# Start of a Mamba mixer and ternary FFN kernel: first x rows as four loads, per-channel constants turned by TensorE, an epsilon added by GpSimd

## What is computed

```
x = x + mixer(hidden=ctx, z=layernorm(x))          # x: (4, 512, 512), ctx: (4, 512, 256), f32
    xc    = depthwise conv, 4 taps, of in_proj_w @ hidden, + conv_b;   u = silu(xc)       (512 channels)
    x_dbl = x_proj_w @ u  ->  dt_lo (16), B (16), C (16)
    delta = softplus(dt_proj_w @ dt_lo + dt_proj_b);   A = -exp(A_log)
    state = state * exp(delta * A) + (delta * u) * B;   y = state . C     (16 states, 512 steps)
    y     = (y + D * u) * silu(z)
x = x + ffn(layernorm(x))                          # activations rounded to 8 bits, weights to -1, 0, 1
    h = silu(x @ gate) * (x @ up);  h = rms_norm(h) * ln_w;  out = h @ down      (512 -> 2048 -> 512)
```

## Time and profile before

| | |
|---|---|
| runs of before | 584.44 us median (584.33 to 585.72, 3 runs) |
| the profiled execution's own time | 582.04 us |
| its span, first to last instruction | 580.1 us |
| busy share of the span | PE 93%, DVE 92%, ACT 88%, POOL 81% |
| transfers over the whole span | 68.64 MB, mean 118 GB/s |

### The profile page before, as it was taken

The page is one execution under the profiler, slowest core; times in us unless marked ns, Lnnn a source line. Parts: engine busy times, 40 slices in busy tenths (PEclk is TensorE's granted clock), DMA queues, the critical chain, the costliest instruction groups (busy, mean ns, idle before and its releaser), DMA issues.

```text
span 580.1 us, 10283 instructions
## 1 busy us (share of the span) xinstructions
PE 539.6 (93%) x3684; PEld 402.7 (69%) x3684; DVE 534.1 (92%) x774; ACT 512.7 (88%) x755; POOL 468.3 (81%) x197
## 2 busy tenths in 40 slices
PE   5898987899999999999999889898989999999996
PEld 2335476899998989989999889886434444444443
DVE  3999989999999999999999999997899989899873
ACT  1899999999999999989999799998877878878784
POOL 4889374999999899999999999994666665765772
PEclk9999999999999999999999899999999999999999
DMA  9992690112113832117331276253453442533521
GB/s 283 407 373 74 217 315 22 55 56 66 63 56 76 180 82 101 55 56 184 109 93 64 61 180 203 66 137 101 73 98 75 89 103 65 108 82 75 117 54 55
DMA packets 62194, 68.64 MB, mean 118 GB/s; under 512 B 41137, under 2 KB 41137, under 8 KB 59969
## 3 DMA queue, kind: packets, MB, share of 16 engines
q1 hardware_dynamic: 59776, 63.59, 36.7%
q0 software_dynamic: 2368, 4.40, 4.6%
HBM read 50.02 MB, written 8.52 MB: 101 GB/s over the span
## 4 chain that ended last, share of the span: by engine, by line
PE 38%; POOL 18%; ACT 17%; DVE 14%; DMA 7%; issue 5%; SPq 0%; DVEq 0%; POOLq 0%
PE ps L1253 16%; POOL arena L471 16%; PE ps L1263 9%; ACT arena L691 8%; ACT arena L616 5%; PE ps L1218 5%; DVE arena L821 5%; DMA arena<-c_rows 4%; PE ps L1202 4%; PE ps L1205 3%; DVE bst_x L853 2%; DMA arena<-x 1%; ACT arena L613 1%; DVE arena L845 1%; DVE wstat L828 1%
## 5 line engine op out<-in xcount | busy, mean ns | idle before, releaser
L471 POOL TENSOR_TENSOR arena<-arena 128x2048 f32<-128x2048 f32 x63 | 286.7, 4609 | 13.3 <-DVE arena L910 9.8
L910 DVE TENSOR_TENSOR_SCAN arena<-arena,ps 128x512 f32<-128x512 f32 x256 | 286.7, 1195 | 1.7 <-DVE var L935 0.5
L691 ACT ACTIVATE arena<-arena,a_neg 128x512 f32<-128x512 f32 x256 | 165.2, 710 | 9.1 <-DVE arena L910 9.0
L1218 PE MATMUL ps<-ident,arena 128*128 128x128 f32 x1024 | 155.3, 275 | 8.2 <-POOL arena L471 5.0
L1218 PEld LDWEIGHTS ps<-ident,arena 128*128 128x128 f32 x1024 | 120.2, 141 | 12.3 <-POOL arena L471 7.7
L1253 PE MATMUL ps<-arena 128*128 128x512 bf16 x512 | 113.5, 379 | 1.4 <-DVE arena L987 0.9
L511 POOL TENSOR_TENSOR arena<-arena 128x1024 f32<-128x1024 f32 x30 | 70.8, 2362 | 49.9 <-DVE arena L987 49.9
L1202 PE MATMUL ps<-arena 128*128 128x128 f32 x768 | 102.4, 276 | 3.0 <-DVE arena L910 2.8
L1205 PE MATMUL ps<-ident,arena 128*128 128x128 f32 x640 | 97.1, 275 | 5.3 <-DVE arena L910 2.9
L616 ACT ACTIVATE arena<-arena,bT 128x512 f32<-128x512 f32 x160 | 102.0, 709 | 0.0
L1202 PEld LDWEIGHTS ps<-arena 128*128 128x128 f32 x768 | 93.3, 192 | 5.0 <-ACT arena L616 1.9
(11 more groups left out here) (118 smaller groups left out, 573.6 us busy)
## 6 DMA issues: line engine op xcount, KB each, us to landing
arena<-w_all SPq DMA_DIRECT2D x16, 1024.0 KB, 9.5
arena<-c_rows SPq DMA_DIRECT2D x64, 256.0 KB, 3.3
arena<-x SPq DMA_DIRECT2D x4, 1024.0 KB, 15.9
w_ternary<-arena SPq DMA_DIRECT2D x8, 512.0 KB, 4.3
arena<-w_ternary SPq DMA_DIRECT2D x8, 512.0 KB, 5.2
arena<-x POOLq DMA_DIRECT2D x4, 1024.0 KB, 10.0
out<-arena SPq DMA_DIRECT2D x16, 256.0 KB, 2.0
arena<-ctx_t SPq DMA_DIRECT2D x4, 512.0 KB, 13.9
```

The costliest lines, as they stand in the source:

```text
L471: nc.gpsimd.tensor_tensor(hs[:, k % RING, :, :], hs[:, k % RING, :, :], c_bc[:, s:s + 1, :].to_broadcast([P, KE, L]), ALU.mult).then_inc(S ...
L691: nc.scalar.activation(dA[:, s, i, :], delta_u[:, b, 0, i, :], ACT.Exp, scale=a_neg[:, i, n:n + 1]).then_inc(S["dA_ready"], 1)
L910: nc.vector.tensor_tensor_scan(out=hs[:, k % RING, i, :], data0=dA[:, k % 2, i, :], data1=ps[:, 4 + i, :], initial=0.0, op0=ALU.mult, op1= ...
L1218: last = mm(ps[:, c, i * P:(i + 1) * P], hs[:, k % RING, i, c * P:(c + 1) * P], ident[:], start=(n == 0 and i == 0), stop=(n == DS - 1), i ...
```

## The change

SP's two loads for `cw` and `cb` go, and x of batch 0 is issued as four transfers of one row tile, each with its own semaphore; DVE's first `x_stats` waits for one row tile at a time. The taps, bias and D are loaded as rows (channel group by channel, long contiguous pieces) by three DMAs that ACT issues, turned by six transposes on PE into PSUM, and copied by DVE into `chan`; `tap_of` picks a column of it. PE runs nine products of ones ahead of its first `conv`, and DVE sets `ones` and `magic` before it zeroes `xp_s` and `dt_s`. The epsilon for the x variance is added by POOL in place of DVE. POOL's small loads move behind `x_power(0)` (xp_t, now one transfer, and dt) and `x_power(2)` (a_log); xp_t lands in `xp_raw`, and POOL copies it into `xp_s`.

```diff
 SP
-            load(cw[:], conv_w.rearrange("(k p) n -> p k n", p=P), "conv_loaded")
-            with nc.allow_non_contiguous_dma("one column for each channel"):
-                load(cb[:], conv_b.rearrange("(k p) -> p k", p=P), "conv_loaded")
-            load_x(0)
+            for k in range(KE):
+                sp.dma_start(x_all[:, k, :], x_v[:, 0, k, :]).then_inc(x0_loaded[k], 16)
 POOL
-            pool.wait_ge(S["started"], 2)
-            load(xp_s[:, :, 0:DR], xp_v[:, :, 0:DR], "proj_loaded")
-            load(xp_s[:, :, B_AT:XD], xp_v[:, :, DR:DR + 2 * DS], "proj_loaded")
...
             def x_power(b):
                 pool.wait_ge(S["x_var"], b + 1)
+                own.done(nc.gpsimd.tensor_scalar(var_x[:, b, :], mv_x[:, b, :, 1], LN_EPS, None, ALU.add))
+                own.wait()
 ...
             x_power(0)
+            load(xp_raw, xp_t.rearrange("(k p) n -> p k n", p=P), "xp_loaded")
+            pool.wait_ge(S["started"], 2)
...
             x_norm(0)
+            pool.wait_ge(S["xp_loaded"], 16)
+            nc.gpsimd.tensor_copy(xp_s[:, :, 0:DR], xp_raw[:, :, 0:DR]).then_inc(S["proj_ready"], 1)
+            nc.gpsimd.tensor_copy(xp_s[:, :, B_AT:XD], xp_raw[:, :, DR:]).then_inc(S["proj_ready"], 1)
             x_power(1)
             x_norm(1)
             x_power(2)
+            load(a_neg[:], a_log.rearrange("(k p) n -> p k n", p=P), "a_loaded")
 ACT
-            act.wait_ge(S["conv_loaded"], 16 * 2)
+            for at, src in ((0, conv_w.rearrange("(k p) n -> k (p n)", p=P)),
+                            (TAPS * P, conv_b.rearrange("(k p) -> k p", p=P)),
+                            ((TAPS + 1) * P, d_skip.rearrange("(k p) -> k p", p=P))):
+                act.dma_start(chan_rows[:, at:at + src.shape[1]], src).then_inc(S["chan_loaded"], 16)
             act.preload_act_table_set("silu_and_others")
+            act.wait_ge(S["chan_ready"], 1)
             last_tap(0, 0)
 DVE
-                nc.vector.tensor_scalar(var_x[:, b, :], mv_x[:, b, :, 1], LN_EPS, None,
-                                        ALU.add).then_inc(S["x_var"], 1)
+                dve.sem_inc(S["x_var"], 1)
 ...
             x_stats(0)
+            dve.wait_ge(S["chan_psum"], 1)
+            nc.vector.tensor_copy(chan[:], ps[:, 7, 0:(TAPS + 2) * KE]).then_inc(S["chan_ready"], 1)
+            dve.wait_ge(S["chan_ready"], 1)
             conv(0, 0)
 PE
+            pe.wait_ge(S["dve_consts"], 1)
+            keep_warm(9)
             pe.wait_ge(S["in_loaded"], 16)
             conv(0, 0)
+            pe.wait_ge(S["consts_set"], 1)
+            pe.wait_ge(S["chan_loaded"], 16 * 3)
+            for i in range(TAPS + 2):
+                rows = chan_rows[:, i:TAPS * P:TAPS] if i < TAPS else chan_rows[:, i * P:(i + 1) * P]
+                last = nc.tensor.transpose(ps[:, 7, i * KE:(i + 1) * KE], rows, ident[0:KE, 0:KE])
+            last.then_inc(S["chan_psum"], 1)
             conv(0, 1)
```

More of the change, by code:

```diff
@@ L141, in mixer_ffn @@
         a_neg = sb("a_neg", [P, KE, DS])
-        cw = sb("cw", [P, KE, TAPS])
-        cb = sb("cb", [P, KE])
-        dsk = sb("dsk", [P, KE])
+        chan_rows = part(160, 3)[0:KE, :]
+        chan = sb("chan", [P, (TAPS + 2) * KE])
         magic, minus_magic = sb("magic", [P, 1]), sb("minus_magic", [P, 1])
@@ L174, in mixer_ffn @@
         wq_dram = nc.dram_tensor("w_ternary", [8, P, INNER], BF16).ap()
[L176 removed]
+        names = """a_loaded proj_loaded proj_ready in_loaded chan_loaded chan_psum chan_ready xp_loaded started consts_set dve_consts
             in_proj_done tap0_done conv_steps u_ready xdbl_psum xdbl_ready
@@ L187, in mixer_ffn @@
         x_loaded = [sem(f"x_loaded{b}") for b in range(NB)]
+        x0_loaded = [sem(f"x0_loaded{k}") for k in range(KE)]
         x1_added = [sem(f"x1_added{b}") for b in range(NB)]
@@ L251, in added, with tap_of @@
             return "p_added", k * 2 + half + 1 - k // DS
+        def tap_of(i, k):
+            return chan[:, i * KE + k:i * KE + k + 1]
         def flat(ap):
@@ L398, in _, with load @@
             own = Steps(pool, S["pool_steps"])
+            def load(dst, src, s):
+                nc.gpsimd.dma_start(dst, src).then_inc(S[s], 16)
             own.done(nc.gpsimd.memset(ident[:], 0.0))
@@ L411, in _ @@
                                     pattern=[[0, 1]], channel_multiplier=1).then_inc(S["consts_set"], 1)
-            def load(dst, src, s):
-                nc.gpsimd.dma_start(dst, src).then_inc(S[s], 16)
-            xp_v = xp_t.rearrange("(k p) n -> p k n", p=P)
-            pool.wait_ge(S["started"], 2)
-            load(xp_s[:, :, 0:DR], xp_v[:, :, 0:DR], "proj_loaded")
-            load(xp_s[:, :, B_AT:XD], xp_v[:, :, DR:DR + 2 * DS], "proj_loaded")
[L420 to L426, removed]
             def x_power(b):
                 pool.wait_ge(S["x_var"], b + 1)
+                own.done(nc.gpsimd.tensor_scalar(var_x[:, b, :], mv_x[:, b, :, 1], LN_EPS, None, ALU.add))
+                own.wait()
                 nc.gpsimd.tensor_tensor(rstd_x[:, b, :], var_x[:, b, :], mhalf[:, 0:KE],
@@ L450, in _ @@
             x_power(0)
+            load(xp_raw, xp_t.rearrange("(k p) n -> p k n", p=P), "xp_loaded")
+            pool.wait_ge(S["started"], 2)
+            for j in range(2):
+                at = j * XD
+                load(dt_s[at:at + DR, j, :], dt_t, "proj_loaded")
+                load(dt_s[at + DR:at + DR + 1, j, :], dt_b.rearrange("(a n) -> a n", a=1), "proj_loaded")
             x_norm(0)
+            pool.wait_ge(S["xp_loaded"], 16)
+            nc.gpsimd.tensor_copy(xp_s[:, :, 0:DR], xp_raw[:, :, 0:DR]).then_inc(S["proj_ready"], 1)
+            nc.gpsimd.tensor_copy(xp_s[:, :, B_AT:XD], xp_raw[:, :, DR:]).then_inc(S["proj_ready"], 1)
             x_power(1)
@@ L457, in _ @@
             x_norm(3)
-            pool.wait_ge(S["consts_loaded"], 16 * 2)
+            pool.wait_ge(S["chan_ready"], 1)
             for k in range(KE):
-                nc.gpsimd.tensor_scalar(skip[:, k, :], ident[:], dsk[:, k:k + 1], None,
+                nc.gpsimd.tensor_scalar(skip[:, k, :], ident[:], tap_of(TAPS + 1, k), None,
                                         ALU.mult).then_inc(S["skip_ready"], 1)
@@ L800, in step @@
                 own.wait()
+            step(nc.vector.memset(ones[:], 1.0))
+            nc.vector.memset(magic[:], MAGIC).then_inc(S["dve_consts"], 1)
             nc.vector.memset(xp_s, 0.0).then_inc(S["started"], 1)
             nc.vector.memset(dt_s, 0.0).then_inc(S["started"], 1)
-            step(nc.vector.memset(ones[:], 1.0))
-            nc.vector.memset(magic[:], MAGIC).then_inc(S["dve_consts"], 1)
             nc.vector.memset(minus_magic[:], -MAGIC).then_inc(S["dve_consts"], 1)
```

19 lines of the change are left out of this document (12 added, 7 removed).

## The result

The changed kernel took 586.12 us in the median of 22 runs (583.33 to 588.26); the kernel before took 583.59 on the same chip (22 runs, 580.51 to 586.70). The ratio is 1.0044, with an interval of 1.003 to 1.0059: slower, by 2.5 us, where I had forecast 1.9 us faster (582.5), and outside my range of 581.8 to 584.8. The profiled execution took 585.70 us.

The account below looks back on a forecast made before the run. The set-up's chain was taken to bound it: x of batch 0, then DVE alone, with PE's slow projection beside it. DVE's gain of 2.0 and ACT's 1.9, the smaller holding, gave 584.44 - 1.9 = 582.5 us, range 581.8 to 584.8.

Parts of the forecast that it names:

- the 9.9 us for the first projection: Set-up, PE: with its clock up when ctx lands, the first projection is ready at 9.9 us instead of 12.39.
- rival 1: Set-up: PE's clock is still low at 6.2 us, DVE's first tap comes at 15.0, total 585.0 us; chance 0.15.
- When x is there: Set-up: x of batch 0 lands at 9.7 us instead of 10.96, DVE's statistics done at 10.8 (10.0 to 11.6).
- rival 2: Set-up transfers: the stream is not faster, the rate dips being start-up and not small pieces; total 583.4 us; chance 0.15.
- When the taps are there: Set-up: after projection, six transposes (0.8 to 1.1 us) and DVE's copy, DVE's first tap starts at 12.1, 1.9 us earlier.
- What the stream gives back: Set-up: x of batch 2 lands 1.2 us earlier (0.9 to 1.7), so the gain stays 1.9 us (1.6 to 2.1).
- The variance: Set-up, DVE: epsilon taken off its chain saves 0.15 us each for batches 1, 2 and 3.
- POOL: Set-up: its 6.3 us of added work costs nothing, covered by the wait before du(0), 8.25 us, shrinking to about 6.

Follow-up runs that it names:

- c1: The kernel before with 24 small products of ones (96 PE instructions) ahead of PE's first projection; ratio 1.0009.
- c3: The changed kernel with 51 small products of ones added, so PE has 256 instructions more than in the kernel before; ratio 1.0005.
- c4: The changed kernel with 14 products of ones ahead in place of nine and 46 small ones behind, 256 PE instructions more than the kernel before; ratio 1.0002.
- b1_pad: The kernel before with DVE's `ones` set first and 12 products of ones ahead of PE's first projection; ratio 1.0049.
- a1_nowarm: The changed kernel without the nine products of ones ahead of the first projection; ratio 1.0047.
- c2_pad128: The kernel before with 24 small products ahead of PE's first projection and 8 ahead of that of batch 2 (128 PE instructions); ratio 1.0014.
- a0_again: The changed kernel once more, unedited; ratio to the kernel before 1.0067.
- a3: The changed kernel with three later groups of six products of ones cut to two each, 48 PE instructions fewer; ratio 1.0015.
- a2: The changed kernel with the three loads of rows issued by SP ahead of x in place of ACT; ratio 1.0075.
- a4: The changed kernel with 14 products ahead in place of nine and seventeen later ones cut, 4 PE instructions more than the kernel before; ratio 1.0022.

## Why the prediction was wrong

**The step that failed.** "From there the scan and the FFN run as they did, so what the set-up gains or loses is carried to the end one for one". It does not hold: of 3.3 us that the span grew, 2.6 arose behind the third mark, and 0.46 in the scan, where POOL got a second wait for `c_rows`, 0.97 us long. The change lengthens PE's program, and the place at which PE's instructions are loaded then lies in other transfers. I had counted instructions by their time only, not by their number; the earlier trace rows gave me a price for the transposes of PE, and the queue q8 stood on the page before with its 30 packets. That a hit lengthens a pair, and that the number of PE's instructions decides on hits, is shown (long pairs, c1, c3). That undoing the shift takes away the loss in the medians is shown for the changed kernel by c3 (1.0005) and c4 (1.0002). That the long pairs are all of it is not: in b1_pad one long pair costs 0.8 of the 2.1 us by which its span grew, the second wait for `c_rows` is 0.6 more, and the rest is open; a1_nowarm has one long pair and 1.0047, c2_pad128 two and 1.0014.

The second step that failed is in the set-up, 1.9 us forecast and none in this profile: the 9.9 us for the first projection, taken up next. The forecast's base was off as well, the other way: 584.44 us from three runs, where the 22 runs of the kernel before have 583.59.

**The clock: rival 1, in part.** I took 9.9 us for the first projection and kept 12.4. The profile has 12.15 (6.78 + 5.37), a0_again 10.36 and c3_after256 10.28. My reason against, "the gap is 1 us behind 4 us of work", was wrong by size: PE could start on ctx at 6.78 us, 0.6 later than before, the nine products ended at 4.83 and not at 5.3, and the gap was 1.94. With nine products the projection was fast behind gaps of 1.30, 1.75 and 1.83 us (a0, a3, c3) and slow behind 1.94 (after) and 1.02 (a2). So the gap alone does not decide: after 1.94 the clock had been up and fell, in a2 it had not risen yet. The Trainium skill, "TensorE: Matmul & The Clock Gate", section "What you observe", gives some 500 ns from run to run for the point of the rise. Here the same nine products begin at 1.17 us each time, and the traces' clock records begin the higher level at 4.00 (c3), 4.12 (after), 4.53 (a3), 5.82 (a0) and 10.33 us (a2): it differs from run to run, and by more than the page says.

**When x is there**: right. Forecast were statistics done at 10.8 (10.0 to 11.6); the profile has 10.45. The second dip of the rate is gone. The first is only smaller: from 4.5 to 7.5 us the eight profiles with the changed loads have 326 to 355 GB/s and the six others 248 to 303, so in this stretch part of rival 2 holds.

**When the taps are there**: right where the clock was up when ctx landed. Six transposes took 0.76 us, a little under my 0.8 to 1.1; DVE's first tap came at 12.13 to 12.35 in the five such profiles (a0, a3, a4, c3, c4), against the 12.1 forecast. The three loads of rows were never what PE waited for.

**What the stream gives back**: right in four of the same five. BN_STATS of batch 2 was forecast near 31.0; it came at 31.02 to 31.13 in four and at 32.12 in c4_after_warm256, where DVE waited for x as in rival 2.

**The variance**: forecast 0.15 us for each batch, and nothing was gained. In the order of time DVE goes from the start of the third aggregation to its next work, the mean of the weights, in 35.70 - 35.22 = 0.48 us before:

```profile
35.22 0.38 DVE L856 BATCH_NORM_AGGREGATE mv_x<-bst_x 128x2 f32<-128x6 f32 x4
35.63 0.17 DVE L858 TENSOR_SCALAR var_x<-mv_x 128x4 f32<-128x4 f32 x1
35.70 0.15 DVE L834 TENSOR_REDUCE wsum<-ps 128x1 f32<-128x4 f32 x1
```

With the increment alone (c3_after256) it takes 34.11 - 33.58 = 0.53:

```profile
33.58 0.38 DVE L864 BATCH_NORM_AGGREGATE mv_x<-bst_x 128x2 f32<-128x6 f32 x4
34.11 0.16 DVE L839 TENSOR_REDUCE wsum<-ps 128x1 f32<-128x4 f32 x1
```

Before, the next instruction started 0.07 us behind the start of the variance, so the 0.17 us were hardly ever waited for; the increment still waits for the aggregation to end. With this, and with small losses later, DVE's lead in c3 shrinks: 1.65 us at BN_STATS of batch 2, 1.59 behind the increment, 1.44 at the first tap of batch 3, 1.38 at the rounding of 68 us and 1.17 at the first copy of 77 us. So the set-up gains 1.17 us at the first decay where everything goes well (89.31), and not 1.9.

**POOL**: covered, though not as costed. Its order of time after:

```profile
56.31 4.77 POOL L462 TENSOR_SCALAR arena<-ident,chan 128x128 f32<-128x128 f32 x4
65.54 4.54 POOL L439 TENSOR_TENSOR arena<-arena 128x2048 f32<-128x2048 f32 x1 [4.46 <-DVE arena L853]
```

The wait before `du` is 4.46 us where I forecast 6, chiefly because the skip matrices took 4.77 us and not 2.36. What was left of the cover, 4.46 us, kept it off the path.

## What to carry to other kernels

Before a program is lengthened or shortened on the engine with the most instructions, read the instruction queues in the profile and see where their packets lie against the short transfers that somebody waits for: here 52 more instructions in the set-up made two pairs of transposes cost 2.1 us some 450 us later, and 204 more took that away. When two versions differ by less than 1%, a third with the same edit and a padded or trimmed program tells the edit from its place. Where PE's clock has to be up when the data lands, keep PE busy up to the latest landing that the traces show: with nine products the projection was fast in three of five executions, with fourteen (gaps of 0.54 us and less) in both that were profiled.

## What the runs showed of the hardware

- **Instructions are loaded while the kernel runs.** They are 16 KB packets on q8, one for about 256 PE instructions: 30 in twelve of the profiles, 31 in the two with 256 instructions more. Most take 0.9 to 1.4 us; one that met a load of `c_rows` at 207 us took 2.74.
- **A pair of DMA transposes is held up by one such packet that starts 2 to 2.9 us behind its own start**: 3.38 us become 4.3 to 4.7, and 5.0 to 5.2 where q14's 8 KB packet meets it too (540.53 us after, 1.8 us long). The data stays the same, 2768 packets. A q14 packet alone made 3.8 us at most, a q8 packet that started 1.2 us ahead of the pair 4.0 (c3, 431.28 us), and that cost nothing further on. Through what the one packet holds up the others, the trace does not say.
- **PE's clock also falls in full work**, to 0.5, one to four times in an execution and at other times in another. Of a0_again, with falls at 542 and 572 us, the stretches:

```profile
539.00:546.00 7.00, 4.52 (x14) 0.76 0.36 44
570.00:577.00 7.00, 5.88 (x31) 0.76 0.00 0
```

  The first of them follows a long pair by less than a microsecond, the second follows none; each costs some 2 us of the 162.75. The falls at 570 and 571 us in a1, a3 and a4 (each with only one long pair, and an end of 158.7 to 159.5) cost nearly as much. What brings these on is open.
- **A GpSimd product with a column of another tile** took 1206 ns for 128x128 where it took 611 before; the column now comes from `chan` (24 wide) in place of `dsk` (4 wide). All eight profiles with `chan` have 4.76 or 4.77 us for the four, all six with `dsk` 2.34 to 2.37. Why was not followed up.
